# A four-layer kernel: a second x1 buffer, the condition of layer 3 as a product by batch, and new instruction orders

## The reference, cut to what matters

```python
# layer 0: AdaLN block, 16 heads of 64;  layer 1: RMS norm + FiLM, one head;
# layer 2: AdaLN block, 16 heads of 8;   each layer ends in an MLP 128 -> 512 -> 128
# layer 3, on its input v = exp_v, with q = the batch's condition:
row_zero = exp_v.sum(-1) == 0
q_exp = jnp.where(row_zero[..., None], 0.0, q[:, None, :])
vcq = jnp.concatenate([exp_v, q_exp], axis=-1)
self_feat = vcq @ W_self.T + b_self          # W_self is 128 x 256
# two graph attentions (16 heads of 8, 20 keys) over self_feat, with masks and
# biases summed from the integer mask, added to self_feat; relu; plus exp_v
```

## Time and profile before

| | |
|---|---|
| time before, median of 3 runs | 1184.86 us (1183.1 to 1186.69) |
| the profiled execution | 1181.46 us, its span 1179.7 us |
| PE busy | 1085.0 us, 92% of the span |
| DVE, ACT, POOL busy | 881.7, 770.1, 435.8 us |
| chain that ended last | PE 68%, DVE 19%, ACT 5%, POOL 4%, issue 3% |
| data moved | 17.35 MB read, 2.10 MB written |

### The profile page before, as it was taken

How to read it: one execution, slowest core, us unless ns; L and a number is a source line. 1 busy time by engine, 2 the same in 40 slices (tenths; PEclk the granted TensorE clock), 3 DMA queues, 4 the chain that set the end, 5 groups by cost and what they waited for, 6 DMA issues and landing times.

```text
span 1179.7 us, 24111 instructions
## 1 busy us (share of the span) xinstructions
PE 1085.0 (92%) x8411; PEld 734.9 (62%) x8411; DVE 881.7 (75%) x2510; ACT 770.1 (65%) x2888; POOL 435.8 (37%) x599
## 2 busy tenths in 40 slices
PE   5898999999999999999999999999989988778675
PEld 4565765776577656676667756766567755546434
DVE  2465767786899687996799788996887678858645
ACT  0655567984788547874789548974678628837712
POOL 1231323431454323542355324541344234515313
PEclk9999999999999989999999999999989999988885
DMA  8000000001000100001000100001000100010000
GB/s 259 2 9 1 11 10 1 10 11 32 1 11 11 32 10 9 2 11 41 1 11 3 39 9 11 2 2 40 1 10 2 41 1 1 2 40 1 1 9 10
DMA packets 21822, 20.98 MB, mean 18 GB/s; under 512 B 1143, under 2 KB 20296, under 8 KB 21448
## 3 DMA queue, kind: packets, MB, share of 16 engines
q1 hardware_dynamic: 18536, 15.26, 4.6%
q10 hardware_dynamic: 3168, 4.19, 1.2%
HBM read 17.35 MB, written 2.10 MB: 16 GB/s over the span
## 4 chain that ended last, share of the span: by engine, by line
PE 68%; DVE 19%; ACT 5%; POOL 4%; issue 3%; DMA 1%; POOLq 0%; DVEq 0%; ACTq 0%
PE bank L1002 11%; PE bank L1021 7%; PE bank L1009 7%; PE bank L1026 5%; PE bank L1047 5%; PE bank L1072 5%; PE bank L1062 5%; PE bank L1056 4%; PE bank L1130 4%; PE bank L1138 3%; PE bank L996 3%; PE bank L1148 2%; PE bank L1220 2%; PE bank L1209 2%; ACT prob_space L932 2%
## 5 line engine op out<-in xcount | busy, mean ns | idle before, releaser
L756 POOL TENSOR_TENSOR fprobs<-fprobs,frinv 128x512 f32<-128x512 f32 x128 | 132.7, 1041 | 249.2 <-DVE frinv L1315 248.3
L932 ACT ACTIVATE prob_space<-bank,negmax 128x128 f32<-128x128 f32 x512 | 181.4, 385 | 34.1 <-DVE negmax L1442 33.9
L868 ACT ACTIVATE fprobs<-bank,fnegmax 128x128 f32<-128x128 f32 x512 | 181.1, 388 | 31.3 <-DVE fnegmax L1310 31.1
L1002 PE MATMUL bank<-fhT,w_qkv 128*128 128x512 f32 x256 | 126.1, 615 | 1.5 <-DVE fv L1324 0.8
L729 POOL TENSOR_TENSOR rstd<-veps,half 128x4 f32<-128x4 f32 x40 | 40.5, 1014 | 208.6 <-DVE veps L1272 173.6
L868 ACT ACTIVATION_READ_ACCUMULATOR fprobs<-bank,fnegmax 128x1 f32 x512 | 116.7, 228 | 0.0
L932 ACT ACTIVATION_READ_ACCUMULATOR prob_space<-bank,negmax 128x1 f32 x512 | 115.7, 226 | 0.0
L1310 DVE TENSOR_REDUCE fnegmax<-bank 128x4 f32<-128x512 f32 x128 | 82.1, 682 | 40.3 <-PE bank L1047 39.8
L1442 DVE TENSOR_REDUCE negmax<-bank 128x4 f32<-128x512 f32 x128 | 82.2, 683 | 22.0 <-PE bank L1130 21.6
L874 ACT ACTIVATE fprobsT<-bank 128x512 f32<-128x512 f32 x128 | 74.5, 605 | 36.5 <-PE bank L1056 36.4
L879 ACT ACTIVATE fk<-bank 128x512 f32<-128x512 f32 x64 | 38.8, 607 | 82.0 <-PE bank L1002 82.0
(11 more groups left out here) (193 smaller groups left out, 2503.6 us busy)
## 6 DMA issues: line engine op xcount, KB each, us to landing
adj<-in_mask_BxSxSx_ik SPq DMA_DIRECT2D x8, 440.0 KB
adj<-in_mask_BxSxSx_ik SPq DMA_DIRECT2D x32, 110.0 KB
x_norm<-in_x SPq DMA_DIRECT2D x8, 256.0 KB, 2.9
x_res<-in_x SPq DMA_DIRECT2D x8, 256.0 KB, 2.8
out<-x_out SPq DMA_DIRECT2D x8, 256.0 KB, 2.3
w_qkv<-in_L_cond_W_qkv ACTq DMA_DIRECT2D x1, 1536.0 KB, 6.9
prob_space<-in_w_mod SPq DMA_DIRECT2D x1, 1024.0 KB
w_up<-in_w_up ACTq DMA_DIRECT2D x1, 768.0 KB, 13.2
```

Of the source, the lines that this page charges most:

```text
L756: pool.tensor_tensor(p, p, wide(frinv[:, u, :], D), ALU.mult).then_inc(fnormed.sem, 1)
L868: ins = act.activation(fprobs[:, u % NP, b, :], P.bank(("S", u))[:, tok(b)], ACT.Exp, bias=fnegmax[:, u, b:b + 1], accum_out=frsum[:, u, b ...
L932: ins = act.activation(probs[:, u % NP, i, :], P.bank(("A", u))[:, tok(i)], ACT.Exp, bias=negmax[:, u, i:i + 1], accum_out=rsum[:, u, i:i ...
L1002: ins = pe.matmul(P.bank(result)[:, :], w, a, start=(i == 0), stop=(i == len(terms) - 1))
```

## The change

Three edits. `x1` becomes two buffers, used in turn by group, and the pair of `order_pairs` now ties back g's `y2` to mid g+2's `down (1, 1)`. The product with the condition leaves `self3`: PE multiplies `w3[1]` with the four condition columns of the group in the step `adj`, into four columns of that bank; DVE copies them to `gcond`, no longer counted in the chain; `qx` is then the finished term, and `self3` on DVE adds bank, bias and `qx` in one instruction. All four strings of `ORDERS` are new.

```diff
-END_LINKS = 12
+END_LINKS = 11
...
-        pairs.append((step_at(b, "y2"), step_at(m2, "down", (1, 1))))
+        if g + 2 < NG:
+            pairs.append((step_at(b, "y2"), step_at(MIDS[g + 2], "down", (1, 1))))
...
-        x1 = sb("x1", [D, G, D])
+        x1 = sb("x1", [D, 2, G, D])
...
# PE
                         for i in range(2):
-                            ins = pe.transpose(P.bank("adj")[:, i * G * NK3:(i + 1) * G * NK3], edge1[:, i, :], ident[0:G * NK3, 0:G * NK3])
+                            pe.transpose(P.bank("adj")[:, i * G * NK3:(i + 1) * G * NK3], edge1[:, i, :], ident[0:G * NK3, 0:G * NK3])
+
+                        ins = pe.matmul(P.bank("adj")[:, 2 * G * NK3:2 * G * NK3 + G], w3[:, 1, :], condT[:, 1, g * G:(g + 1) * G], start=True, stop=True)
                         ins.then_inc(P.full_sem("adj"), 1)
...
                     elif what == "self3":
-                        linear(P, "self3", [(w3[:, 0, :], x3T[:, :]), (w3[:, 1, :], qx)], after=["sum3"])
+                        linear(P, "self3", [(w3[:, 0, :], x3T[:, :])])
...
# DVE (x1 becomes x1[:, g % 2, :, :] in add, stat, unit and y2)
-                        dve.tensor_copy(gcond[:, :], condT[:, 1, bass.ds(g * G, G)]).then_inc(chain.sem, 1)
-                        dve.wait_ge(*chain.last(g))
                         dve.wait_ge(*P.full("adj"))
+                        dve.tensor_copy(gcond[:, :], P.bank("adj")[:, 2 * G * NK3:2 * G * NK3 + G])
...
-                        biased(P, "self3", sT[:, :], ROW["L3_cond_b_self"])
+                        c = ROW["L3_cond_b_self"]
+                        dve.wait_ge(*P.drained("sum3"))
+                        dve.wait_ge(*P.full("self3"))
+                        dve.scalar_tensor_tensor(sT[:, :], P.bank("self3")[:, :], col[:, c:c + 1], qx, ALU.add,
+                                                 ALU.add).then_inc(P.free_sem("self3"), 1)
```

More of the change, by code:

```diff
@@ new lines @@
+            "UUdNUGUHHdHGVHVHVeHeOHHOVVVHeVHVOVeOeeOVHHOVVOVVOHHVHOHOHeVVVHeHVHHVHHVOVVHVeHeVVVeVOeVHOHHOOHeVHVHV"
+            "HHeHVHHHOVOHVHHVVOVVHHHVHOOeHVHOHHVeHHVHHHeHHHVVHOHOVVHOVHVHHHHVVHOeWfHfHHHHWHHWfHWfPWPWPfWfPPfWWPWW"
+            "WPWPPPWWWWWfWWPWWfPWPPPfWfWWPWWWfPWWPWfPWWWfWWPWWfPfWWfWPWPfPWWWWPWWWWXgXgXgXXXXXgXXXXXggXXXXXgXXXXg"
+            "XgXXXXXXXgXXXXXXgXXgXXgXXgXgXgXgXXgXXXXhhhhhhhhhhhhhhhhhh"),
+        "DVE": (
+            "AAAAAAAAAAAAAAAAAAAAAAAAAAAAAAAAAAAAAAAAAAAAAAAAAAAAAAAAAAAAAAAAAAABAAAAAAABAAIBBBBIBBBIIBBBBBBIBIBB"
+            "IBBBBIBBIBBBIBIBBBBBIBIIIBBBBBBBIBIBBBBBBBBIIBBBBIBIBBBBBBBBBBBBBCCBIBBBIIIQCCBBCCBCCCBJCCCJCQCJCQCC"
+            "CJJQQQQCQCJQCQCJQQQQJCJCCQCJCCQCCQQCCCCQJQCCQQCCCQCQJJQQQQJCCCCJQJCQCQJCQCJJCCQQQCCCQQQCJQCCQJCCQCCQ"
+            "CCJCQQJCCCCQCJCJCCQQCCCCCQDKQQQRDDRDDRaDDaDRaRRKDRaRRDRKRaaDDRRKRDKKRKDDDaRDDDKDRRRDDKDRDRDRDDaDDRDR"
+            "KDaDRDRDKDDDaDKRRRKRRDRKDRDDDDKaDKDaDDDDRKRDRRKDDKDRRDDKDDRDDaKRDDDDKDaKDRDDRRDaDDKRRaDRDRDDaKDRLRaR"
+            "SEESEEEbSEEbEELSbSSLSLSLSSEbbESESESSSEbLLbEEEEEESESSLSELSEESSSEESbEEEEEELbSEEESELEEbSLSELSSLSEEELSEb"
+            "EEbEEEESSLLEEESSESLLESESSEEbELEEESELLEEbEEESEESSSEEbSEELLESbSELEbMSMSSTbFFTFFTcFFFFccTTTMFTTFcMcTTTT"
+            "MTFMFTFTMFccTFFFFMFFTFFTFTMTFTFTFFcFFFTMFTFcTFFFTTFMFTFFFcTMTTMMFFTMcFFTFMFcFFTMFTFTTFMTFFMFFTFTFFMF"
+            "FFcFMFFMFTFFFTcTTFMFFTFTMTcFFMFTcTTccTFGUGGUGUNGGdUdGNGdGUUUNUdUUGddUNUGUGNGUUNNGGdGUNGUGGUUGGUNGGGU"
+            "GUNGGdGGGUNdGUUGUUNGGUdGGGUGUGUNGNGUGNUdNGGGdGGGGNGUUUGUUNGGGNGGUUGGGNGddGGUGGNGGUdGGUUUGUNGGGNNUdUG"
+            "GdNGUUUHVHHVdGHHOHVHeHVeVVOVHeHVVOOeVVOeeHHVOVHOHOVHVHOeHVVVOHeVHHVHHHVVOVVeHeVVVHVeOeHOHHOHVeOVHOVV"
+            "VHHHeHHHHVOVHHVeVHVVOOHVHHHHeOVHOHHVHHHHVHeVHHHOHVHVHVHeHHHHHVVOHVVffOHHOHHWHWHWHfPfWPWPPWfWPfWPWWWf"
+            "WWPPWWPWPWWWWfPWWWPWffPPfPWWPWWWfPWWPWWfPWWfWWPfWPWPWfWWfWWWWWWWWWPPfPXXXggXXXXgXXgXXXXgXgXXXgXXXXgX"
+            "XgXXXXXXXXXXgXXXXXgXgXgXgXgXXgXgXXXXXXghhhhhhhhhhhhhhhhhh"),
@@ L1421, in mid @@
                         dve.wait_ge(*xb_ready.nth(g, 1))
[L1422 removed]
+                        add(P, "g1", x1[:, g % 2, :, :], mz)
                     yield
@@ L1451, in back @@
                                               ALU.mult).then_inc(biasg_ready.sem, 1)
-                        stat(BACK, g, k, x1 if k == 4 else x)
+                        stat(BACK, g, k, x1[:, g % 2, :, :] if k == 4 else x)
                     elif what == "unit":
-                        unit(BACK, g, k, x1 if k == 4 else x)
+                        unit(BACK, g, k, x1[:, g % 2, :, :] if k == 4 else x)
                     elif what == "turn":
```

97 lines of the change are left out of this document (39 added, 58 removed).

## The result

The changed kernel takes 1168.51 us (median of four runs, 1160.71 to 1174.43), the kernel before 1183.98 in the same comparison (1182.25 to 1186.69). The ratio is 0.9867, with an interval of 0.983 to 0.9904. That is 15.5 us less; forecast were 9.3 less, with a time of 1175.6 and a range of 1168 to 1188. Measured again later, beside other runs of the kernel before, it took 1171.69 (seven runs, 1159.36 to 1179.55), ratio 0.9877 [0.9839, 0.9916]. That ratio leaves out the slowest of the seven, which is over 1.5% above the fastest.

What follows compares the result with a forecast made beforehand. PE was taken as the bound in the dense part, chains through several engines in the last part. 3.3 + 2.3 + 1.7 + 1.95, about 9.3 us saved, gave 1175.6 us on the median's scale, range 1168 to 1188.

Steps and rivals of the forecast that it cites:

- The wait at self3: Dense part, 120 to 1000 us: PE's two waits for `qx` go and PE ends earlier by the full 2.3 us.
- Group h: Tail, last group: first product runs during `qx`, so `sT` starts earlier; 1.95 us saved.
- The narrow product: `self3` of groups a to f: four-column product replaces a full one, 0.55 us saved each, 3.3 us in all.
- the first rival: Dense part: PE's gain returns as longer waits for DVE, ACT or POOL; 1182.9 us, no change; chance 0.18.
- Group g: Thin part, X's start: new order moves `self3`'s products out of a full PE stretch; 1.7 us saved.
- The new strings: All instruction orders: 0 beyond the counted terms; bounds 5.8 us gain, 15.6 us loss.
- The bound of 5.8: Dense part: most that orders could gain, from L838's 3.6 and `km`'s 2.2 us waits; all won, 1169.8 us, chance 0.13.
- The second x1: x1 buffer in all groups: orders never use the second early, so 0; at most 1.3 us of gain.
- km: Ahead of `S2 0` in R, S, T, V: less work covers PE's `km` wait, 8.8 us loss, 1184.4 us; chance 0.06.
- The clock in X's stretch: 1060 to 1076 us: PE's 15.56 us of work runs at 1.2 GHz, taking twice as long; 1191.2 us; chance 0.13.

Runs made afterwards that it cites:

- edit 2 alone: The kernel before with only the narrow condition product replacing self3's second product, old orders and single x1: 1177.78 us, ratio 0.9958.

## Why the prediction was right, and where it was wrong

The direction and the range held; the time was 7 us under the forecast, on the low end. By its own steps:

**The wait at self3, 2.3 us: wrong, though the total seems to fit.** Keeping only the wait costs 3.7 to 4.1 us, about what the dense waits and the tail's share were to give. But of the two dense waits the one at d (0.66) is still there with edit 2 alone, and the one at e (1.59) gives back at most 0.25: PE waits as long for `vm` and `prob_space` instead. My step that PE ends earlier by the full wait, since the work behind it was due anyway, is what failed. The measured 3.7 to 4.1 lie behind 944 us, in the tail and in the clock.

**Group h, 1.95 us: right.** `sT` came 2.05 us earlier behind `qx`, and the stretch to the last output is 2.2 us shorter.

**The narrow product, 3.3 us: the price right, the effect wrong.** It costs 0.32 us, and PE lost the work that I gave. But putting a full product back changes no median in either order, taking it out without the wait gives 0.9993, and of the work in three groups 0.44 to 1.12 us of 2.6 come through. PE's idle time shows the exchange: between a's `x3T` and f's it is 16.8 us before and 18.5 with edit 2 alone, although e's wait of 1.6 for `qx` is gone from it. That is 3.3 us more of other waits. It is the first rival's mechanism, "hidden anyway". My argument against it, that PE is at 98%, was the step that failed: a busy share says how little idle time there is, not that the next instruction was ready when PE asked. Yet edit 2 alone gives 5 to 6 us. The tail's 2 and the 1 or 2 of the product are placed; the rest is not.

**Group g, 1.7 us: wrong.** The order did what I read in it: the wait for z fell from 6.2 to 3.9. From `x3T` of g to `x3T` of h it is 84.2 us, against 84.6 before, at a mean clock of 0.80 and 0.82. The clock moves this stretch by more than the 1.7: it took 87.5 us at 0.75 in the changed kernel's second profile and 79.7 at 0.87 in that with a single x1.

**The new strings, 0: wrong in size.** Given edit 2 they are worth 6 to 11 us (0.9958 to 0.9867 and 0.9877 is 11 and 10; 9.3 and 6.1 by the medians). Without it they cost 6 to 7. The bound of 5.8 was read from two waits of the trace: `p` (L838), which in the dense part went from 3.6 to 1.1, and `km`, from 2.2 to 0.7, 4.0 us together. So a bound from two wait rows was too tight. 3.3 us of the gain lie between a's `x3T` and d's, at full clock; how much of the rest is the clock's stays open.

**The second x1, 0: right**, as is the count that no order uses it.

**km: wrong rival, and no loss.** Its wait fell to 0.7 us although less stands between `kq2` and `S2 0`. The row of 2.2 us was about something else, below.

**The clock in X's stretch: did not decide, but it moves.** It stands at 1.00 from 1060 to 1068 us and at 0.76 to 1076 in the changed kernel's profile, so part of that stretch did slow down, but not the 15.6 us of work that the rival needed.

So the forecast came near by luck, by errors against each other: 7.3 us for PE work and dense waits that were worth an estimated 1 or 2, and 0 for strings that were worth 6 to 11. Only the tail's 1.95 holds as it was argued.

## What to carry to other kernels

Before counting an engine's saved time, look a few us downstream for its next wait: if one stands there for another engine, the saving ends in it, even on an engine at 98%. This holds for a removed wait as for removed work: the wait of 1.59 us at group e gave back 0.25 at most, while three waits at the same line under the new strings, 7.3 us together, cost their full length. To place a gain, compare the start of one marked instruction per group in two profiles: stretches at full clock repeat here to 0.1 us, where the medians of whole runs leave 2 or 3 us open. Strings and edits that were made for each other have to be priced together: one half alone made this kernel slower.

## What the hardware showed beside that

**DVE stands still beside POOL.** The same four `mz` instructions (128x128, from SBUF to SBUF) take 3.95, 3.17 or 1.38 us. DVE and POOL in the kernel before, in the changed kernel, and in the one with the added product:

```profile
429.15 3.95 DVE L1280 TENSOR_SCALAR mz<-x_res,mv,rstd 128x128 f32<-128x128 f32 x4
433.02 0.74 DVE L1373 TENSOR_SCALAR qk<-bank,col 128x512 f32<-128x512 f32 x1
...
428.99 1.04 POOL L793 TENSOR_TENSOR km<-qk,head 128x512 f32<-128x512 f32 x1 [7.40 <-ACT qk L898]
429.99 2.04 POOL L756 TENSOR_TENSOR fprobs<-fprobs,frinv 128x512 f32<-128x512 f32 x2
431.98 1.04 POOL L793 TENSOR_TENSOR km<-qk,head 128x512 f32<-128x512 f32 x1
```

```profile
424.30 3.17 DVE L1283 TENSOR_SCALAR mz<-x_res,mv,rstd 128x128 f32<-128x128 f32 x4
424.78 2.04 POOL L794 TENSOR_TENSOR km<-qk,head 128x512 f32<-128x512 f32 x2
```

```profile
425.33 1.38 DVE L1285 TENSOR_SCALAR mz<-x_res,mv,rstd 128x128 f32<-128x128 f32 x4
...
426.49 2.12 POOL L794 TENSOR_TENSOR km<-qk,head 128x512 f32<-128x512 f32 x2 [0.63 <-ACT qk L899]
```

In the first, POOL works from 428.99 to 433.02 without a break, and each `mz` takes as long as one of POOL's (0.99 against 1.04). In the last, the first `mz` takes 0.61, until POOL's instruction of before has ended, and the other three, with POOL idle for 0.63, some 0.34 each. PE's 2.21 us wait in the kernel before, put down to `km`, ended at 433.87, just behind DVE's query scaling L1373 (to 433.76), which stood behind `mz`; POOL's last `km` had ended at 433.02. The Trainium skill ("SBUF — State Buffer", section "🔬 SBUF: two separate sides") describes the port pair that DVE and POOL share as a lock that the instruction that starts first holds to its end; the 3.95 against 1.38 us agree. At this place it also explains where the product's time went: PE is held up where DVE waits for POOL, and with the product `mz` happens to fall into a gap of POOL's. That the other groups go the same way was not looked at one by one.

**The clock varies by itself.** Executions of one kernel differ by up to 20 us and go with their granted clock, by 0.12 to 0.34 us per us at 1.2 GHz. So a part of a 5 us difference between two medians can be the clock's. Windows around group b's `self3` in the kernel before, and with edit 2 alone:

```profile
425.00:435.00 10.00, 7.79 (x30) 4.04 (x28) 9.83 (x27) 3.40 (x15) 4.60 (x5) 0.97 0.01 2
435.00:445.00 10.00, 10.00 (x35) 6.43 (x34) 6.66 (x14) 5.08 (x26) 1.72 (x5) 0.52 0.00 0
```

```profile
420.00:430.00 10.00, 7.92 (x39) 4.73 (x39) 9.86 (x25) 4.95 (x20) 4.24 (x5) 1.00 0.01 2
430.00:440.00 10.00, 10.00 (x54) 5.96 (x51) 7.67 (x20) 8.56 (x32) 4.79 (x13) 1.00 0.00 1
```

PE is idle 2.2 and 2.1 us in the two; in one profile the clock drops to 0.52 in the next 10 us of full work, in the other it stays at 1.00. So after the same kind of gap 10 us of work run at half clock in one profile and at full clock in the other. These are one execution of each, and of two kernels; that one program differs from run to run by this is likely, and not shown.
